# A fused decoder layer on one core: value products of attention in three fp32r parts instead of one fp32 product, for 536 of 1088 tiles

## The reference, cut to what matters

```python
x = layernorm(x + mamba(x, ...))                 # 4 x 512 rows of 256, 512 inner channels, 16 states
x = layernorm(x + cross_attention(ctx, x, ...))  # 16 heads of 64; 4 batches
x = layernorm(x + experts(x, ...))               # 2 shared and 8 routed experts, top 2

# cross_attention, for each batch:
q = layer_norm(x) @ Wq                           # 512 queries
k, v = split(concat(layer_norm(ctx), layer_norm(x)) @ Wkv)   # 1601 + 512 = 2113 keys
w = softmax(q_scaled @ k_scaled.T)               # per head: 512 x 2113
out = (w @ v) @ Wout                             # "value product": w @ v
```

## Time and profile before

| what | value |
|---|---|
| median of three runs | 3115.12 us |
| the profiled execution: time | 3116.32 us |
| the profiled execution: span | 3114.6 us |
| before the first slot of attention | 310 us |
| batches 0, 1, 2 of attention (16 heads each) | 597 us each |
| batch 3 of attention | 559 us |
| experts and the end | 454 us |
| PE, DVE, ACT, POOL busy over the span | 95%, 63%, 43%, 35% |

### The profile page before, as it was taken

One profiled execution on the slowest core, in us unless ns is written; L12 is line 12 of the kernel. 1 busy time (PEld: TensorE's weight loads), 2 busy tenths in 40 slices (PEclk: granted clock), 3 DMA queues, 4 the chain that ended last, 5 costly groups with the idle time before them and its releaser, 6 DMA issues. The chain is left out here.

```text
span 3114.6 us, 33965 instructions
## 1 busy us (share of the span) xinstructions
PE 2951.2 (95%) x11610; PEld 1849.9 (59%) x11610; DVE 1951.6 (63%) x3381; ACT 1347.4 (43%) x2318; POOL 1084.6 (35%) x850
## 2 busy tenths in 40 slices
PE   7577999999999999999999999999999999899996
PEld 3234565656565656566666666665656565676665
DVE  5897777775667777756777775655555454452225
ACT  4653545453545454435454554454343434211121
POOL 4495667660017675500466663000000000102213
PEclk9898999999999999999999999999999999799998
DMA  6352312111122121201221122101010100411112
GB/s 221 145 180 92 92 35 59 35 56 52 38 69 65 35 58 35 82 18 51 70 65 58 35 62 59 38 13 40 15 38 14 38 15 14 169 60 51 55 43 68
DMA packets 71679, 189.84 MB, mean 61 GB/s; under 512 B 8420, under 2 KB 39272, under 8 KB 63448
## 3 DMA queue, kind: packets, MB, share of 16 engines
q1 hardware_dynamic: 67096, 172.08, 18.2%
q0 software_dynamic: 3984, 15.60, 1.6%
q10 hardware_dynamic: 432, 0.01, 0.0%
HBM read 124.59 MB, written 28.44 MB: 49 GB/s over the span
## 5 line engine op out<-in xcount | busy, mean ns | idle before, releaser
L1100 ACT ACTIVATE a_carry<-a_st 128x512 f32<-128x512 f32 (+1 forms) x1088 | 649.4, 597 | 1125.5 <-PE a_st L1528 1117.1
L1540 PE MATMUL a_o<-a_carry,a_vals 128*65 128x512 f32 (+1 forms) x2176 | 1113.7, 593 | 0.0
L1277 DVE TENSOR_REDUCE a_maxes<-a_mx 128x1 f32<-128x512 f32 x1016 | 678.0, 686 | 224.6 <-PE a_mx L1451 217.1
L1528 PE MATMUL a_st<-a_q,a_kone 65*128 65x512 f32 (+1 forms) x1088 | 431.9, 397 | 0.0
L961 POOL TENSOR_TENSOR a_shared<-a_shared,a_bc 128x512 f32<-128x512 f32 x192 | 251.6, 1311 | 385.1 <-DVE a_shared L1217 385.1
L1540 PEld LDWEIGHTS a_o<-a_carry,a_vals 128*65 128x65 f32 (+1 forms) x2176 | 284.2, 137 | 103.7 <-issue 1.8
L1527 PE MATMUL a_st<-a_q,a_keven 128*128 128x512 f32 (+1 forms) x544 | 326.1, 599 | 1.4 <-ACT a_q L1079 0.9
L932 POOL TENSOR_TENSOR a_erstd<-a_emv,a_half 128x4 f32<-128x4 f32 x7 | 7.1, 1014 | 892.4 <-DVE a_emv L1303 892.4
L1527 PE MATMUL a_st<-a_q,a_kodd 128*128 128x512 f32 (+1 forms) x544 | 314.9, 579 | 0.0
L1451 PE MATMUL a_mx<-a_kodd,a_q 128*128 128x512 f32 x512 | 298.1, 598 | 9.2 <-DVE a_maxes L1277 8.3
L1217 DVE TENSOR_TENSOR_SCAN a_shared<-a_shared 128x512 f32<-128x512 f32 x192 | 288.5, 1505 | 14.5 <-POOL a_shared L950 13.1
(11 more groups left out here) (267 smaller groups left out, 4437.6 us busy)
## 6 DMA issues: line engine op xcount, KB each, us to landing
a_bc<-m_kept_bc SPq DMA_DIRECT2D x48, 512.0 KB, 3.7
a_wt<-a_w_split SPq DMA_DIRECT2D x15, 1536.0 KB, 9.1
a_kone<-a_keven SPq DMA_DIRECT2D x32, 528.5 KB, 4.5
a_kone<-a_kodd SPq DMA_DIRECT2D x32, 528.5 KB, 4.3
e_wall<-in_w_t_dram SPq DMA_DIRECT2D x27, 512.0 KB, 9.8
a_shared<-m_kept_bc SPq DMA_DIRECT2D x16, 512.0 KB, 3.6
a_w_split<-a_wt POOLq DMA_DIRECT2D x4, 1536.0 KB, 6.3
a_shared<-in_ctx_dram SPq DMA_DIRECT2D x4, 1536.0 KB
```

The source lines that it names most:

```text
L1100: nc.scalar.activation(p_of(s % 4)[0:r], st[0:r, s % 2], ACT.Exp, scale=SCALE).then_inc(exp_done, 1)
L1277: nc.vector.reduce_max(maxes[:, c, t:t + 1], mx_bank(g, i), AX_X).then_inc(mx_max, 1)
L1528: nc.tensor.matmul(st[0:r, s % 2], k_one[g % 2][0:DH + 1, kt * P:kt * P + r], qm[of(g)][0:DH + 1, :], start=False, stop=True).then_inc(st_ ...
L1540: nc.tensor.matmul(ps_o[0:DH + 1, g % 2], vals[0:r, kt * HG + j, :], p_of(s % 4)[0:r], start=(kt == 0), stop=(kt == KT - 1)).then_inc(pv_d ...
```

## The change

**Value products.** For some tiles (`is_split`) the fp32 product is replaced by three fp32r products into the same PSUM bank: high values x high exponentials, low values x high exponentials, high values x low exponentials. Per head: all 17 tiles in batch 3 (272 tiles); tiles 0 to 9 in heads 12 to 15 of batches 0 to 2 (120 tiles); tiles 1, 5, 9 and 13 in heads 0 to 11 of batches 0 to 2 (144 tiles).

**Parts of the exponentials.** After each exponential of such a tile ACT waits for its own result and copies it to fp32r (the high part). The low part (exponential minus high part, two SBUF inputs) is written by POOL in batch 3 and in heads 12 to 15, and by DVE ("R", two slots after the tile) for the 144 tiles. PE's third part waits for the low part.

**Parts of the values.** Where a tile is split, ACT writes the high part from PSUM and DVE the low part, in place of DVE's copy; in the first stage of attention this takes the place of ACT's own copy.

**What follows from the space.** The parts lie over buffers of mamba that are idle by then. So the output's and Wout's buffers become single, Wout's load stands at slot 10 of every fourth head, and the load of a following batch's dt and dt*x (`load_batch`) waits, from the second such load on, for the last value product of the batch before; the units of that scan begin 6 slots later.

**Convolution.** In `prepare` the last tap is multiplied by ACT straight from PSUM (16 more instructions of 128 x 512); DVE does three taps instead of four (its 16 TENSOR_SCALARs go, the 48 others stay).

```diff
@@ prepare
+                    act.wait_ge(xs_ready, i * CT)
                 for c in range(CT):
                     wait_full(act, ("x", i, c))
+                    nc.scalar.activation(cv[:, c], bank(("x", i, c)), ACT.Copy, scale=cw[:, c, DC - 1:DC])
                     nc.scalar.activation(xs_pad[:, c, DC - 1:], bank(("x", i, c)), ACT.Copy).then_inc(front_read, 1)
...
-                    if j == 0:
-                        ins = nc.vector.tensor_scalar(cv[:, c], tap, w, None, ALU.mult)
-                    else:
-                        ins = nc.vector.scalar_tensor_tensor(cv[:, c], tap, w, cv[:, c], ALU.mult, ALU.add)
+                    ins = nc.vector.scalar_tensor_tensor(cv[:, c], xs_pad[:, c, j:j + S], cw[:, c, j:j + 1], cv[:, c],
+                                                         ALU.mult, ALU.add)
@@ beside
+FEW = (1, 5, 9, 13)
+def unit_slot(b, u):
+    return int(u * U_STEP) + (6 if b > 0 else 0)
...
+    if g < (B - 1) * H and h < H - HG:
+        for kt in FEW:
+            at[kt + 2].insert(0, ("R", g, kt))
+LAST = (B - 1) * H
+SOME = 10
+def is_split(g, kt):
+    return g >= LAST or kt < SOME and g % H >= H - HG or kt in FEW and g % H < H - HG
+def by_dve(g):
+    return g < LAST and g % H < H - HG
@@ SP, load_batch
                 sp.wait_ge(turned_low, b * len(PREP))
+                if b > 1:
+                    sp.wait_ge(pv_done, (b - 1) * H * KT)
@@ POOL
+            def low_exp(g, kt):
...
+                pool.wait_ge(p_high_ready, SPLIT[g, kt] + 1)
+                nc.gpsimd.tensor_tensor(p_low(g, kt)[0:r], p[0:r], p_high(g, kt)[0:r].bitcast(F32),
+                                        ALU.subtract).then_inc(p_low_pool, 1)
@@ ACT, exp
                 nc.scalar.activation(p_of(s % 4)[0:r], st[0:r, s % 2], ACT.Exp, scale=SCALE).then_inc(exp_done, 1)
+                if divmod(s, KT) in SPLIT:
+                    act.wait_ge(exp_done, s + 1)
+                    nc.scalar.activation(p_high(*divmod(s, KT))[0:r], p_of(s % 4)[0:r], ACT.Copy).then_inc(p_high_ready, 1)
@@ DVE
+            def low_exp(g, kt):
+                dve.wait_ge(p_high_ready, SPLIT[g, kt] + 1)
+                nc.vector.tensor_tensor(p_low(g, kt), p_of((g * KT + kt) % 4), p_high(g, kt).bitcast(F32),
+                                        ALU.subtract).then_inc(p_low_dve, 1)
@@ PE, add_o
+                if (g, kt) in SPLIT:
+                    high, low = vals_high[0:r, kt * HG + j, :], vals_low(g // HG)[0:r, low_place(g // HG, kt) + j]
+                    pe.wait_ge(p_high_ready, SPLIT[g, kt] + 1)
+                    nc.tensor.matmul(ps_o[0:DH + 1, g % 2], high, p_high(g, kt)[0:r], start=(kt == 0), stop=False)
+                    nc.tensor.matmul(ps_o[0:DH, g % 2], low, p_high(g, kt)[0:r], start=False, stop=False)
+                    wait_low(pe, g, kt)
+                    nc.tensor.matmul(ps_o[0:DH + 1, g % 2], high, p_low(g, kt)[0:r], start=False, stop=(kt == KT - 1)).then_inc(pv_done, 1)
+                    return
```

More of the change, by code:

```diff
@@ L620, with has_split, low_place @@
 BANK, RANK = ring_banks()
-HIGH = {x: i for i, x in enumerate(x for x in MADE if x[0] in "QK")}
+LAST = (B - 1) * H
[4 more added lines that the diff above has]
+    return g < LAST and g % H < H - HG
+SPLIT, SPLIT_POOL, SPLIT_DVE = {}, {}, {}
+for tile in ((g, kt) for g in range(NH) for kt in range(KT) if is_split(g, kt)):
+    own = SPLIT_DVE if by_dve(tile[0]) else SPLIT_POOL
+    SPLIT[tile], own[tile] = len(SPLIT), len(own)
+def has_split(what):
+    t, w = VB[what[2]] if what[0] == "V" else (0, 0)
+    return any(is_split(what[1] * HG, kt) for kt in range(t, t + w))
+def low_place(n, kt):
+    return HG * (FEW.index(kt) if by_dve(n * HG) else kt)
+HIGH = {x: i for i, x in enumerate(x for x in MADE if x[0] in "QK" or has_split(x))}
 POW = {x: i for i, x in enumerate(x for x in MADE if x[0] in "EGLg" or x[0] == "A" and x[2] == 1)}
@@ L1087, in make @@
                     turned_rows_high(what)
-                elif what[0] == "V" and what in BEFORE:
+                elif what[0] == "V" and what in BEFORE and not has_split(what):
                     values(what)
@@ L1313, in make @@
                 kind = what[0]
-                if kind == "V" and what in BEFORE:
+                if kind == "V" and what in BEFORE and not has_split(what):
                     return
@@ L1484, in project_out @@
                 wait_bank(what)
-                nc.tensor.matmul(ring[:, bank(what), 0:DM + 1], o_sb[0:DH + 1, g % 2, t * P:(t + 1) * P],
-                                 wo_sb[0:DH + 1, g // HG % 2, g % HG], start=True, stop=True).then_inc(ring_full, 1)
+                nc.tensor.matmul(ring[:, bank(what), 0:DM + 1], o_sb[0:DH + 1, t * P:(t + 1) * P],
+                                 wo_sb[0:DH + 1, g % HG], start=True, stop=True).then_inc(ring_full, 1)
             def sum_state(u):
```

103 lines of the change are left out of this document (79 added, 24 removed).

## The result

The changed kernel takes 3121.52 us (median of 10 runs, 3119.92 to 3124.32) against 3114.18 us (10 runs, 3111.09 to 3118.14) for the kernel before. The ratio is 1.0023, with a 95% interval of 1.0015 to 1.0032. The profiled execution has a span of 3118.6 us (3114.6 before). I had forecast 3095. The time lies inside my range, but its sign is the other one.

A forecast was written before the change was run, and what follows sets the result against it. Attention was taken as bound by PE's issue. The terms -35.5 - 12.5 + 7.5 + 20 + 0.5 = -20 us gave 3096 us against the profiled execution, 3095 against the median; range 3064 to 3134.

The forecast's parts named there:

- What bounds it: Attention: bound by what PE issues, slot after slot; PE busy 95% of the span.
- what a tile gains: Each split tile: three parts take 0.705 us for an fp32 product's 0.86, saving 0.155 us; 83 us over 536 tiles.
- rival 3: Parts cheaper on PE, 0.216 us each: 21 us more saved where PE is the bound, 3075 us; chance 0.06.
- Batch 3: All 272 tiles of batch 3: -42.2 + 1.7 + 5 = -35.5 us, bounds -42 and -20.
- My loss for the last head: Last head of batch 3: POOL and ACT want 1.27 us a slot against 1.17, so 1.7 us are lost.
- Head 14: Head 14 of batches 0 to 2, 30 tiles: ACT's copies add 2.5 us a head, +7.5 us in all.
- Heads 12, 13 and 15: These heads of batches 0 to 2, 90 tiles: POOL has room after the scan; -12.5 us.
- The shift: Scan units beginning 6 slots later in batches 1 and 2: given no price of its own.
- the late load: dt loads from batch 2 on, landing after the first unit is due: +0.5 us each, +1 in all.
- The 144 tiles: Tiles with DVE's low parts, heads 0 to 11 of batches 0 to 2: 1.1 us a part, +2.3 a group, +20 us.
- the evictions of V: First stage of attention: DVE gets six more evictions of V, half a microsecond each, +2.5 us.
- Rival 2: Heads 0 to 10, slots 3 to 13: DVE becomes the bound; 3132 us at 1.5 us a low part; chance 0.22.

The follow-up runs named there:

- last_only: Changed kernel with three-part products in batch 3 alone, units not shifted, dt load not waiting for value products: 3079.36 us, ratio 0.9886 to the kernel before.
- some_shift0: Changed kernel without the 144 tiles with DVE's low parts, dt load released after tile 9 of head 15, units not shifted: 3089.53 us, ratio 0.9926.
- v_first: Changed kernel with early dt load and no shift (3112.7 us), evictions of V put ahead of the scan's unit in each group's first head: 3110.22 us.
- no_few: Changed kernel without the 144 tiles that have DVE's low part; late dt load and shift stay: 3098.52 us, ratio 0.995 to the kernel before.

## Why the prediction was wrong, step by step

**What bounds it, and what a tile gains: right.** With five fp32r matmuls to a slot in the last head (timeline of PE, the answer to the earlier trace rows):

```profile
2655.40 0.40 PE L1647 MATMUL a_st<-a_q,a_kodd 128*128 128x512 f32 x1
2655.64 0.39 PE L1648 MATMUL a_st<-a_q,a_kone 65*128 65x512 f32 x1
2655.86 0.39 PE L1662 MATMUL a_o<-a_phigh,a_valshigh 128*65 128x512 f32 x1
2656.09 0.39 PE L1663 MATMUL a_o<-a_phigh,a_lowlast 128*64 128x512 f32 x1
2656.32 0.40 PE L1665 MATMUL a_o<-a_plow,a_valshigh 128*65 128x512 f32 x1
2656.56 0.39 PE L1647 MATMUL a_st<-a_q,a_kodd 128*128 128x512 f32 x1
```

A slot is 1.16 us and a matmul 0.232, against my 0.235. Third heads of batch 3 get 2.83 us shorter, 0.166 a tile where I had 0.155. The Trainium skill (TensorE: Matmul & The Clock Gate, Back-to-back issue gap) would have 0.216 us; the rows disagree, and rival 3 falls with it.

**Batch 3: right, -32.7 for -35.5.** My loss for the last head was too large: it saves 2.9 us, not 0.9. Its late slots take 1.16 us, where I let ACT and POOL hold them at 1.27. Four slots before them take 1.60 us (2648.54 to 2654.70), in which POOL catches up; from 2656.24 its subtractions follow each other 1.25 us apart, the three slots of lag take up the difference, and only the last two value products wait for it, which costs 0.3 us behind the last slot. The fourth heads save only 1.25 and the first 2.2, where I had 2.0 and 2.6. ACT is 411.2 of 525.9 us busy, 78%.

**Head 14: near in size by luck, +9.1 for +7.5; the wait was another.** The window of slots 0 to 9 (changed kernel, batch 1), beside head 14 in the earlier trace rows:

```profile
1443.42:1467.28 23.86, 20.66 (x95) 13.47 (x94) 20.67 (x36) 21.24 (x40) 12.71 (x9) 1.00 0.09 19
```

ACT is the fullest engine, 21.24 us, close to my 22.1, and the slots take 23.86 us where I had 23.3. But PE's idle 3.2 us are no waits for ACT. The waits of that window (PE, line, released by: us, times, longest) hold one entry of PE for nearly all of it. Below it stands the timeline at the longest of them, and last the same pair of normalisations in last_only:

```profile
PE a_ring L1503 <- DVE a_shared L1295: 3.1, 3, 1.5
...
1452.15 3.12 POOL L1016 TENSOR_TENSOR a_plow<-a_carry,a_phigh 128x512 fp32r<-128x512 f32 x2 [0.98 <-ACT a_phigh L1204]
1452.77 2.66 DVE L1295 TENSOR_SCALAR a_shared<-a_shared,a_mv,a_rstd 128x256 f32<-128x256 f32 x2
1455.48 0.66 PE L1503 MATMUL a_ring<-a_ident,a_shared 128*128 128x128 f32 x4 [1.52 <-DVE a_shared L1295]
...
1428.23 0.73 DVE L1293 TENSOR_SCALAR a_shared<-a_shared,a_mv,a_rstd 128x256 f32<-128x256 f32 x2
```

DVE's two row normalisations take 0.73 us with POOL idle and 2.66, 1.70 and 1.69 us ahead of PE's three waits, beside POOL's subtractions; DVE is busy 20.7 us in place of 16.4 with no work added to it. It is the same meeting as in head 13 of some_shift0, and the loss that I had put on ACT is made by the step that failed for head 13, named next. That it would go with POOL's subtractions out of the way was not tested.

**Heads 12, 13 and 15: the first step that failed, about 0 for -12.5.** (+0.6 in some_shift0; -2.8 in the changed kernel, whose heads 13 kept more of the clock.) Head 12 did save 1.7 us. Head 13 cost 1.6 to 3.2 in place of saving 1.3, since "POOL has finished the scan, so its subtractions have room" looked at POOL alone. Its subtractions have room, but DVE's work has less beside them. I had weighed that sharing for the scan and dropped it where there is no scan. In the changed kernel head 13 costs +0.3, +1.65 and +1.65; windows of its first and second (stretch, us, busy of PE, granted clock):

```profile
792.39:830.66 38.27, 35.63 (x147) 1.00 0.19 59
1403.75:1443.42 39.67, 37.03 (x147) 0.96 0.19 57
```

PE waits 2.54 and 2.55 us in the two, and yet one has a clock of 1.00 and the other of 0.96, and they differ by 1.4 us. With the clock at 0.92 it is 3.2. The traces hold 24 heads 13 with such a wait of 2.53 to 2.56 us: the head's clock is 1.00 in 4 of them, 0.96 in 10 and 0.92 in 10. This is why head 13 doesn't repeat from kernel to kernel. Why the clock falls at some of these equal waits and not at others no run here tells. Head 15 saves half of what I had; its rest was not traced further than to slot 2, where the exponential comes 0.6 us later behind Q's copies.

**The shift: the second step that failed, 7 to 9 us for nothing.** I priced the late load at +1, which fits the runs (0 by the medians, 2.3 by the heads of the traces), and the 6 slots of the units at nothing. They are 2.1 units, so that POOL's products meet scans which they had missed before, as the place in head 25 shows.

**The 144 tiles: right in sum, +22 for +22.5 (with the evictions of V), by two errors.** A low part takes 1.04 us on average (I had 1.1). But an ordinary group of four costs 1.0 to 1.7 us without the shift, not 2.3: second heads +1.5 and +2.0, third +0.7 and -0.3, fourth -0.4. The first group of a batch costs 8, 5 and 4 us, where I had 2.3 each and 2.5 more in batch 0. In batch 0 nearly 4 of it is the chain of V parts behind the decay (v_first). In batches 1 and 2 that reordering left the loss; there 2.4 and 1.6 us of it stand at slot 3 of heads 17 and 33, and in head 17 PE waits 2.3 us for DVE's low part of Q. What delays that part was not tested. Rival 2's rule, that DVE takes over in second heads, holds as a mechanism, but its price of 1.5 us a part was not reached.

**The sum.** Measured by the runs, partly from traces and partly from ratios (the 144 tiles and the convolution): -32.7 (batch 3) - 2.7 (put to the convolution, not shown) + 0.6 (heads 12, 13, 15) + 9.1 (head 14) + 1.4 (head 11) + 22.4 (144 tiles) + 7.5 (shift and load: no_few against some_shift0) = +5.6, against +7.3 measured. The forecast of -20 lacked 13 in heads 12, 13 and 15, 7 in the shift, and a few in batch 3 and head 14. I had called it wrong if batches 0 to 2 moved by more than 15 us each; they moved by 11.0, 15.7 and 15.4.

## What to carry to other kernels

Splitting a product so that PE has less to do pays only where PE is the engine that is waited for; here batch 3 alone, with an idle POOL and room on ACT, gives 33 us, and the other 264 tiles, as they were arranged, cost 42 more than they saved; with one group of normalisations moved, 120 of them came near to costing nothing. Price a new instruction not only by its own engine's room but by what it does to the other engine that shares its port, and look there for the longest wait that PE already has: lengthened, it can take the clock with it. A shift of periodic work is a change of its own; shift by a whole period of what it meets, or price each meeting.
